# A two-layer attention and mixture-of-experts kernel: register loads at the head of the routed blocks grouped, block counts kept for four blocks, and the order of some steps moved

## What is computed

```python
x = x + L0_xattn_ref(layernorm(x), ctx, ctx, ...)   # softmax attention, 16 heads of 8
x = x + L0_ffn_ref(layernorm(x), ...)               # top 2 of 8 experts, silu(g) * v, hidden 256
x = x + L1_xattn_ref(layernorm(x), ctx, ...)        # linear attention: softmax features, kv product
x = x + L1_ffn_ref(layernorm(x), ...)               # 2 shared experts (mean) + top 2 of 8, gelu, hidden 512
```

## Time and profile before

| | |
|---|---|
| median of 3 runs | 716.31 us (714.04 to 717.26) |
| the profiled execution | 716.5 us |
| its span, first to last instruction | 714.5 us |
| mean granted TensorE clock | 0.966 |
| first layer's blocks on PE | about 263 to 386 us |
| second attention on PE | about 386 to 559 us |
| second layer's blocks on PE | 562 us to the end |

### The profile page before, as it was taken

One profiled execution on the slowest core, in us unless ns is written; L12 is line 12 of the kernel. 1 busy time (PEld: TensorE's weight loads), 2 busy tenths in 40 slices (PEclk: granted clock), 3 DMA queues, 4 the chain that ended last, 5 costly groups with the idle time before them and its releaser, 6 DMA issues.

```text
span 714.5 us, 15805 instructions
## 1 busy us (share of the span) xinstructions
PE 655.3 (92%) x5160; PEld 494.1 (69%) x5160; DVE 452.1 (63%) x1336; ACT 340.4 (48%) x739; POOL 383.2 (54%) x502
## 2 busy tenths in 40 slices
PE   6999999999998879999998899999998799999991
PEld 3556666665667669899997455556554599999990
DVE  2577788788877757786778568776564133333433
ACT  3444454454443244444666466766543354544440
POOL 5312255765746744555677566676645145545552
PEclk9999999999999689999999999999999999999997
DMA  6831112112210167888882300000001888888875
GB/s 178 238 61 11 8 20 30 34 19 29 36 26 24 55 174 220 248 260 265 253 262 84 100 31 27 23 30 27 31 21 52 237 272 261 264 261 268 278 232 165
DMA packets 102120, 91.36 MB, mean 128 GB/s; under 512 B 52952, under 2 KB 85848, under 8 KB 101720
## 3 DMA queue, kind: packets, MB, share of 16 engines
q1 hardware_dynamic: 88487, 69.85, 35.4%
q0 software_dynamic: 8640, 17.84, 7.1%
q10 hardware_dynamic: 4913, 2.67, 1.4%
HBM read 69.14 MB, written 22.72 MB: 129 GB/s over the span
## 4 chain that ended last, share of the span: by engine, by line
PE 65%; DVE 14%; SPq 5%; issue 5%; ACT 4%; DMA 3%; POOL 2%; POOLq 0%; DVEq 0%; ACTq 0%
PE pair L1543 37%; PE pair L1877 11%; PE pair L1546 8%; PE pair L1941 5%; DVE sm L1272 4%; DVE smax L1268 4%; PE pair L1668 2%; PE pair L1683 2%; DMA xr<-xs_sorted 1%; SPq L500 1%; SPq L504 1%; POOL xs_sorted L615 1%; SPq L493 1%; ACT L924 1%; SPq L494 1%
## 5 line engine op out<-in xcount | busy, mean ns | idle before, releaser
L689 POOL DMA_INDIRECT y_tok<-ysb,xr x142 | 138.8, 978 | 123.7 <-DVE ysb L1149 58.5
L615 POOL DMA_INDIRECT xs_sorted<-xa,slot_i x128 | 131.5, 1027 | 86.2 <-DVE slot_i L1055 50.9
L1543 PE MATMUL pair<-xT,w_all 128*128 128x256 f32 (+1 forms) x640 | 139.3, 362 | 0.0
L1543 PEld LDWEIGHTS pair<-xT,w_all 128*128 128x128 f32 x640 | 109.7, 196 | 9.6
L1877 PEld LDWEIGHTS pair<-w_all,hT 128*128 128x128 f32 x852 | 107.6, 194 | 6.0 <-issue 2.8
L1877 PE MATMUL pair<-w_all,hT 128*128 128x128 f32 x852 | 109.3, 277 | 2.2 <-DVE hT L1135 1.9
L873 ACT ACTIVATE hT<-pair,w_all 128x256 f32<-128x256 f32 (+1 forms) x160 | 62.5, 448 | 74.5 <-PE pair L1543 73.8
L1127 DVE COPY xT<-pair 128x256 f32<-128x256 f32 (+1 forms) x80 | 31.4, 393 | 95.2 <-PE pair L1546 91.5
L937 ACT ACTIVATE hS<-pair,w_sh 128x512 f32<-128x512 f32 x64 | 44.0, 687 | 60.5 <-PE pair L1543 59.7
L1543 PE MATMUL pair<-xeT_all,w_sh 128*128 128x512 f32 x128 | 68.6, 619 | 0.0
L1941 PE MATMUL pair<-hS,w_sh 128*128 128x512 f32 x128 | 66.4, 602 | 0.0
(11 more groups left out here) (222 smaller groups left out, 1090.3 us busy)
## 6 DMA issues: line engine op xcount, KB each, us to landing
w_all<-in_w SPq DMA_DIRECT2D x40, 578.0 KB, 4.3
w_all<-in_w SPq DMA_DIRECT2D x40, 450.0 KB, 3.9
xa<-y_tok SPq DMA_DIRECT2D x32, 256.0 KB, 4.3
xr<-xs_sorted SPq DMA_DIRECT2D x62, 130.0 KB, 3.3
y_tok<-ysb,xr POOLq DMA_INDIRECT x142
xs_sorted<-xa,slot_i POOLq DMA_INDIRECT x128, 2.3
xs_sorted<-in_pads SPq DMA_DIRECT2D x12, 130.0 KB, 3.9
xr<-xs_sorted SPq DMA_DIRECT2D x18, 65.0 KB, 2.6
```

Source lines behind the costliest of these rows:

```text
L615: g.indirect_dma_start(xs_dram[l], bass.IndirectOffsetOnAxis(ap=slot_i[:, i:i + 1], axis=0), xa[:, GT * c + j // TOPK, j % TOPK, :], None)\
L689: g.indirect_dma_start(y_dram[l], bass.IndirectOffsetOnAxis(ap=xr[u % NXR][:, t, P:P + 1].bitcast(I32), axis=0), ysb[u % NYB][:, t, :], None)\
L1543: return mm(out_, l_, r_, start=True, stop=True)
```

## The change

1. SP's numbers for the first blocks of a layer: the expert numbers of 5 blocks, the rows of 6 and the counts of 6 are read by three grouped loads ahead of the first DMA, each value still being checked; the eight ends of the experts come by one load. From the seventh block on each number is read as before.
2. `NEARLY_B` goes from 12 to 4: from the fifth block on no count is used, and the fifth block waits for the full value of `sorted`.
3. All eight pad DMAs are issued by SP, none by ACT.
4. ACT, beside the first layer's blocks: `up(u)`, `gate_rows(u-2)`, `beside(u)` in place of `beside(u)`, `gate_rows(u-2)`, `up(u)`.
5. The shared half steps: line 1 holds ten numbered steps (ups 0 to 4, downs 0 to 3) in place of eight, and each later line is one pair ahead (-6 in place of -8).
6. PE in line 1: `out_turned` and `project` stand earlier, `ranks` at the end; `project(1)` also waits for the logits of group 0, now counted by `lg_ready`. In line 8 `shared_turn` stands behind `list_order`.
7. DVE: the sum into `bias[:, 5]` stands ahead of the last three `context_shift`.

```diff
-NEARLY_B = 12
+NEARLY_B = 4
 def shared_step(u, k):
-    at = (k if k % 2 else k // 2) if u == 1 else 16 * (u - 1) - 8 + k
-    return divmod(at, 2) if u > 1 or k % 2 == 0 else (-1, 0)
+    at = 16 * (u - 1) - 6 + k
+    if u == 1:
+        at = {0: 0, 1: 1, 2: 2, 3: 3, 4: 4, 5: 5, 8: 6, 9: 7, 12: 8, 13: 9}.get(k, -1)
+    return divmod(at, 2)
...
-                def block_weights(u):
+                def block_weights(u, e=None):
                     after(sp, S("y_sum"), u - NWB + 1)
-                    e = sp.value_load(e_i[0:1, 0, u - u0:u - u0 + 1], min_val=0, max_val=E - 1)
+                    if e is None:
+                        e = sp.value_load(e_i[0:1, 0, u - u0:u - u0 + 1], min_val=0, max_val=E - 1)
...
-                def block_rows(u):
+                def block_rows(u, r=None, count=None):
...
+                    if u < u0 + NEARLY_B and count is None:
+                        count = sp.value_load(e_i[0:1, 2, u - u0:u - u0 + 1], min_val=1, max_val=3)
                     if u < u0 + NEARLY_B:
-                        count = sp.value_load(e_i[0:1, 2, u - u0:u - u0 + 1], min_val=1, max_val=3)
                         sp.wait_ge(S("sorted"), count)
...
-                for k in range(0, E - 3):
-                    tail_rows(k)
+                _, ends = nc.values_load_multi_w_load_instructions(tail_i[0:1, 0:E], engines=[sp.engine], min_val=0,
+                                                                   max_val=(E - 1) * PITCH + NTOK)
+                for k in range(E):
+                    sp.dma_start(xs_dram[l][bass.ds(ends[k], P), :], a["pads"][k * P:(k + 1) * P, :])\
+                        .then_inc(S("xs_padded"), 16)
                 sp.wait_ge(S("emap"), l + 1)
                 sp.wait_ge(S("blocks_padded"), 16 * 2 * -(-SPARE // BLK))
+                _, first_e = nc.values_load_multi_w_load_instructions(e_i[0:1, 0, 0:NWB], engines=[sp.engine], min_val=0, max_val=E - 1)
+                _, first_r = nc.values_load_multi_w_load_instructions(e_i[0:1, 1, 0:AHEAD], engines=[sp.engine], min_val=0,
+                                         max_val=E * PITCH + SPARE - 2 * P)
+                _, first_n = nc.values_load_multi_w_load_instructions(e_i[0:1, 2, 0:AHEAD], engines=[sp.engine], min_val=1, max_val=3)
                 for k in range(AHEAD):
                     if k < NWB:
-                        block_weights(u0 + k)
-                    block_rows(u0 + k)
+                        block_weights(u0 + k, first_e[k])
+                    block_rows(u0 + k, first_r[k], first_n[k])
...
-                for k in range(E - 3, E):
-                    tail_rows(0, k)
...
                     for u in range(NB + 2):
-                        beside(u)
+                        if u < NB:
+                            up(u)
                         if u >= 2:
                             gate_rows(u - 2)
-                        if u < NB:
-                            up(u)
+                        beside(u)
...
-                for g in range(5, NGRP):
-                    context_shift(g)
                 dve.wait_ge(S("bv_done"), 2)
                 dve.wait_ge(S("bias_in1"), 16 * 3)
                 v.tensor_tensor(bias[:, 5, :], bank[5][:, 0:P], bias[:, 5, :], ALU.add).then_inc(S("bias1_ready"), 1)
+                for g in range(5, NGRP):
+                    context_shift(g)
...
             def project(u):
                 pe.wait_ge(S("oT_ready1"), u + 1)
+                if u == 1:
+                    pe.wait_ge(S("lg_ready"), NGRP + 1)
...
+                    if u == 1:
+                        out_turned(u)
                     fill(8, 9)
                     if u == 1:
-                        out_turned(u)
+                        project(u)
                     if live(u - 1):
                         after(pe, S("sx_added"), u - 2)
                         column_sums(1, u - 1)
                     fill(10, 11)
                     if u > 1 and live(u):
                         out_turned(u)
-                    if u == 1:
-                        project(u)
-                    if live(u - 1):
+                    if u > 1 and live(u - 1):
                         ranks(1, u - 1)
                     fill(12)
                     if u > 1 and live(u):
                         project(u)
-                    if live(u - 2):
+                    if live(u - 2) and u != NGRP:
                         shared_turn(u - 2)
                     fill(13)
                     if u == NGRP:
                         list_order(1)
+                        shared_turn(u - 2)
...
                     fill(15)
+                    if u == 1:
+                        ranks(1, u - 1)
```

More of the change, by code:

```diff
@@ L489, in routed @@
                 wc = (W0C, W1C)[l]
-                def block_weights(u):
+                def block_weights(u, e=None):
                     after(sp, S("y_sum"), u - NWB + 1)
-                    e = sp.value_load(e_i[0:1, 0, u - u0:u - u0 + 1], min_val=0, max_val=E - 1)
+                    if e is None:
+                        e = sp.value_load(e_i[0:1, 0, u - u0:u - u0 + 1], min_val=0, max_val=E - 1)
                     sp.dma_start(w_blk[u % NWB][:, 0:wc], wsrc[bass.ds(e, 1)].rearrange("o p c -> p (o c)"))\
                         .then_inc(S(f"w_in{u % NWB}"), 16)
-                def block_rows(u):
+                def block_rows(u, r=None, count=None):
                     after(sp, S(f"y_out{u % NYB}"), stored(u - NXR + NYB))
                     n = tiles_of(u)
-                    r = sp.value_load(e_i[0:1, 1, u - u0:u - u0 + 1], min_val=0, max_val=E * PITCH + SPARE - n * P)
+                    if r is None:
+                        r = sp.value_load(e_i[0:1, 1, u - u0:u - u0 + 1], min_val=0, max_val=E * PITCH + SPARE - n * P)
                     if u == u0 + NFRONT:
                         sp.wait_ge(S(f"rows{l}"), TOPK * 16 * (NT - GT))
+                    if u < u0 + NEARLY_B and count is None:
+                        count = sp.value_load(e_i[0:1, 2, u - u0:u - u0 + 1], min_val=1, max_val=3)
                     if u < u0 + NEARLY_B:
-                        count = sp.value_load(e_i[0:1, 2, u - u0:u - u0 + 1], min_val=1, max_val=3)
                         sp.wait_ge(S("sorted"), count)
@@ L748, in norm_input @@
                 last.then_inc(S(f"xn_ready{l}"), 1)
-            def tail_rows(l, k):
-                act.wait_ge(S("tails"), l + 1)
-                r = act.value_load(tail_i[0:1, k:k + 1], min_val=0, max_val=(E - 1) * PITCH + NTOK)
-                act.dma_start(xs_dram[l][bass.ds(r, P), :], a["pads"][k * P:(k + 1) * P, :]).then_inc(S("xs_padded"), 16)
             def context_values(g):
@@ L957, in attention1 @@
                     gelu(u, 2)
-                    if u == NGRP + 1:
-                        tail_rows(1, 5)
                     if live(u) and u > 1:
@@ L965, in attention1 @@
                     gelu(u, 4)
-                    if u == NGRP + 1:
-                        tail_rows(1, 6)
                     if live(u) and u > 1:
@@ L972, in attention1 @@
                         second_copy(u - 1)
-                    if u == NGRP + 1:
-                        tail_rows(1, 7)
                     if live(u + 1):
@@ L1285, in logits @@
                     v.tensor_copy(lg[:, GT * u:GT * (u + 1), :], bank[logit_bank(u)][:, 0:GT * E].rearrange("p (t e) -> p t e", e=E))\
-                        .then_inc(S("lg_ready0"), 1)
-                    dve.wait_ge(S("lg_ready0"), u + 1)
+                        .then_inc(S("lg_ready"), 1)
+                    dve.wait_ge(S("lg_ready"), u + 1)
                 def output(u):
@@ L1459, in logits @@
                 dve.wait_ge(S("logit_done1"), u + 1)
-                link(v.tensor_tensor(lg[:, GT * u:GT * (u + 1), :],
-                                     line_bank("logits", u)[:, 0:GT * E].rearrange("p (t e) -> p t e", e=E),
-                                     rb[:].unsqueeze(1).to_broadcast([P, GT, E]), ALU.add))
+                v.tensor_tensor(lg[:, GT * u:GT * (u + 1), :],
+                                line_bank("logits", u)[:, 0:GT * E].rearrange("p (t e) -> p t e", e=E),
+                                rb[:].unsqueeze(1).to_broadcast([P, GT, E]), ALU.add).then_inc(S("lg_ready"), 1)
+                dve.wait_ge(S("lg_ready"), NGRP + u + 1)
             def output(u, steps=(0, 1)):
@@ L1695, in expand @@
                     if u != U_LAST:
-                        after(pe, S("lg_ready0"), u)
+                        after(pe, S("lg_ready"), u)
                     for t in range(GT):
```

3 lines of the change are left out of this document (removed).

## The result

The changed kernel took 736.13 us (median of 4 runs, 734.15 to 738.61) against 716.21 for the kernel before in the same session: ratio 1.0284, interval 1.0244 to 1.0324. The forecast was 731.0 with a range of 720 to 738: right in sign and main mechanism, 5.1 us short. The profiled execution took 735.57 us, its span 733.5, 19.0 longer than before, at a mean granted clock of 0.965 (0.966 before).

The account below looks back on a forecast made before the run. PE's own queue was taken as the bound (busy 92% of 714.5 us). Terms 10.5 + 1.5 + 3.2 - 1.0 + 0.5 = +14.7 us on the median of 716.31 gave 731.0 us, range 720 to 738.

Parts of the forecast that it names:

- Pair steps: Second attention, lines 2 to 8: PE's down waits for ACT's copy, seven times 1.5 us, +10.5 us.
- Line 1: First line of the second attention: project waits longer for ACT's oT copy, +1.5 us, bounds 0 and +3.
- may come back cold: First line of the second attention: PE, after waiting longer, may resume at a lower clock; no separate price.
- ACT's order: Beside the first layer's blocks: PE waits for ACT's delayed side work, +3.2 us, bounds +1 and +5.
- u = 39: End of the first layer's blocks: hT comes earlier, one table load goes, Exp later; some 0.4 us gained.
- SP's head: Start of each block stage on SP: three loads and 17 checks before the first weights, taken as 5.3 us.
- level at the sixth block: Block stages: PE opens 2 to 3 us late but is bound by weights landing, so even by block six.
- the two fronts: Opening of the block stages: first layer -1.0 us, second +0.5, bounds -2 and +4 each.
- The tails on SP: Eight tail DMAs on SP instead of five: 8.7 us, done before SP's next step, costing nothing; margin 0.9 us.
- the pair step costs nothing: Rival, second attention: ACT's copy is already done, so 10.5 us goes and 721 is left; 8%.
- Each register costs a load of its own: Rival, SP's block-stage start: grouped loads save nothing, 9.5 us in place of 5.3, total 735; 18%.
- The faster rival: Stage order costs nothing and waits for rows go, 708 to 712 us, if SP's first weights come early; 8%.

Follow-up runs that it names:

- undo_steps: The changed kernel with the old numbering of the shared half steps and PE's old order in lines 1 and 8: 724.93 us, ratio 1.0115 to before.
- undo_act: The changed kernel with ACT's old order beside the first layer's blocks (beside, gate_rows, up): 732.69 us, ratio 1.0231 to before.
- head_only: The kernel before with the new SP block-stage start alone (grouped loads, NEARLY_B = 4, eight tails on SP, bias sum moved): 719.74 us, ratio 1.0054.
- best_d: The kernel before with NEARLY_B = 4 and grouped loads, their eleven checks left out, the first weights' DMA ahead of the other loads: 712.90 us, ratio 0.9946.
- copy_first: The changed kernel with ACT's copy of the finished group (shared_out) ahead of its gelu of k=8: 728.72 us, ratio 1.0184 to before.

## Why the prediction was right, point by point

**Pair steps, +10.5: right, 11.3.** The step names the down, the copy behind its gelu, seven lines and 1.5 us; the trace has the same down, seven waits and 1.61. Undoing the steps gave back 11.2 by the median, and moving the copy 11.24 in the segment of the periods. I took 0.08 off for overlapping activations; the trace has 0.11 of overlap, but also 0.14 from the copy's end to the down, which I had left out. The 0.28 of the earlier trace rows is no measure of it: PE was busy with the step ahead of that down. Left out too were 0.5 us for the slower steps behind the seven stands.

**Line 1, +1.5: right in size, 1.2.** undo_steps has the same order of ACT and the old line 1. From the turn of u = 29 to the Exp of line 2 it takes 65.02, the changed kernel 65.65: 0.63. Another 0.6 falls behind the Exp, where I said that PE "may come back cold" without a price: it does, at a granted clock of 0.50. (The +1.43 of the table compares two traces that reach line 1 at different times.)

**ACT's order, +3.2: right in place, a little dearer, about 3.9.** The wait for lent at u = 29 is 1.29 in place of 0.17, 1.1 as worked out. From there to the Exp of line 2 undo_steps takes 65.02 and the kernel before 62.27: 2.75 more. The median of undo_act gave back 3.4. To the first shared up the table has 1.10 and 1.95, 3.05 together and very near to 3.2, but that is luck: the trace of before lost about 1.7 there to the clock, and against head_only and best_d, which did not, the second term is 3.6. PE's up(39) starts at 384.56 in place of 380.06, 4.50 late where my terms up to there say 3.6. u = 39 itself, where I had a gain of 0.4, gives nothing back at the same clock: from up(39) to the first shared up 8.67, against 8.46 in head_only and best_d and 10.12 in the kernel before. The table load of 1.28 had the Exp right behind it again (387.06 + 1.28, Exp at 388.36), with nothing in between.

**SP's head: this step failed.** I took a load of six for the price of one, 0.3; it is 0.73, so the head takes 7.0 and not 5.3. That sits between my value and the 9.5 of single loads, and nearest to the estimate of 7.8 worked out with the figure of the Trainium skill (Runtime: NRT & Kernel Launch, Instruction fetch mechanics). But the trace doesn't bear out its 200 ns per register, given there for loads from HBM: from one to five registers the load grows by 0.38, some 0.1 each, and the rest of the head is checks.

Second, "it is level at the sixth block" held in neither layer. In the first, copy_first's sixth up comes 24.6 us behind e_i and that of before 22.4; level they are at the thirteenth (43.4 both), and there the kernels with NEARLY_B = 4 and a short head are some 2 us ahead. I put the two fronts at -1.0 and +0.5; by the segments of this pair of traces they cost +1.5 (2.58 less the 1.10 of u = 29) and +2.2. The +1.5 is that execution's: the three other kernels with the same first front have +0.9 to +1.2 in place of 2.58, which is the 1.10 and a front of about 0. head_only has +0.5 and +3.0.

Third, "The tails on SP: nothing" rested on 0.9 us of margin. The 8.7 for the tails was right (8.85), but in the second layer e_i came 1.34 sooner behind tail_i by the new line 8 (7.13, against 8.49 in undo_steps), which I had put at nothing; so the margin wasn't there, and the head began 1.0 late.

**The sum.** +14.7 was forecast for a span that grew by 19.0: 12.3 for 10.5 in the periods (0.8 a mis-sized stand, 0.5 the steps behind the stands, 0.5 in the first period), 3.7 for -0.5 in the two fronts (some 1.5 of it in this execution alone), 4.5 for 4.7 in ACT's order and line 1 together (3.05 and 1.43), and -1.5 upstream that no kernel explains.

**The rivals.** That the pair step costs nothing is refuted by undo_steps. "Each register costs a load of its own" is refuted by the rows, though its time, 735, is nearer to the result than mine. The faster rival had its place right: the head decides, and it wants the first weights early. In the change they come 7.9 and 8.5 us behind e_i in the two layers, before 1.6; best_d keeps 1.6, brings the later pairs closer and gets 3.9 us, NEARLY_B = 4 included.

## What to carry to other kernels

When a step that frees or claims a buffer is moved on one engine, walk the other engine's queue up to the copy that must come between, with all that stands ahead of it: here one place further on PE cost 11 us, and moving the copy ahead of a norm of 1.6 us gave nearly all of it back. Group register loads behind the first DMA that needs one of them and not ahead of it, and count the checks: here they were twice as dear as the loads. Before you read a loss from one trace, see where that execution lies among the others and what clock it was granted: undo_act's trace was the slowest of four, and its half clock looked like a cost of the order of steps.

## What the runs showed that I had not expected

- A register load's price grows with its registers, but slowly: 0.27 for one, 0.54 for eight (560.28), 0.61 to 0.65 for five, 0.72 to 0.74 for six. Eight at once, from another tensor, were cheaper than five; why, no run here shows.
- A bounds check costs 0.25 us a value on SP, almost as much as a load of one. Eight unchecked tails start 2.0 us sooner.
- SP's DMA issues with a register address from the grouped load stand 0.52 apart for weights and rows, and 0.70 for the tails.
- The first 250 us vary by up to 3.9 us from one profiled execution to the next (e_i at 251.4 to 255.3), while the segment of the periods came to between 132.63 and 132.69 in all seven kernels that have the pair steps of before. So a segment of such a stage can be compared to tenths of a us between two traces. Others can't: e_i to the turn of u = 29 came to 95.89 to 97.58 in four kernels that are the same there.
- Behind the same wait of 1.9 for hT the granted clock fell to half in two traces (before, undo_act) and stayed at 1.00 in two (head_only, best_d). It was worth 1.7 us up to the first shared up. Between kernels with line 1 as before most of it was gone at the Exp of line 2: 62.27 before, 62.13 in head_only, 62.07 in best_d.
